# A conditioned block in fp32: two expert halves on VectorE, the second norm on ScalarE, pair sums and the last residual on GpSimd, and orders written out engine by engine

## The reference, cut to what matters

```python
mod = (_silu(L0_c) @ L0_wmod).reshape(8, 6, 1, -1)       # sa, ca, ga, sb, cb, gb per batch
ga = (2 * (ga >= 0) - 1) * jnp.maximum(jnp.abs(ga), 0.25)
gb = (2 * (gb >= 0) - 1) * jnp.maximum(jnp.abs(gb), 0.25)
h = _layernorm(x) * (1 + ca) + sa
# mixer: v, gate = split(h @ W_in + b_in); hs = scan(sigmoid(A) * hs + v); y = sigmoid(gate) * hs * C
x = x + ga * (y @ W_out + b_out)
h = _layernorm(x) * (1 + cb) + sb
# router: softmax(h @ gate_w + gate_b), weights under 0.1 dropped, the rest made to sum to 1
# experts: sum over 8 of weight[e] * (h @ expert_w[e] + expert_b[e])
x = x + gb * experts
```

## Time and profile before

| | |
|---|---|
| median of 3 runs | 230.62 us (230.43 to 231.8) |
| the profiled execution | 229.9 us, span of its instructions 227.9 us |
| VectorE busy | 210.7 us (92%) |
| TensorE busy | 205.3 us (90%) |
| ScalarE busy | 172.8 us (76%) |
| GpSimd busy | 155.7 us (68%) |
| granted TensorE clock, mean | 0.975 of 2.4 GHz |

### The profile page before, as it was taken

How to read it: one execution, slowest core, us unless ns; L and a number is a source line. 1 busy time by engine, 2 the same in 40 slices (tenths; PEclk the granted TensorE clock), 3 DMA queues, 4 the chain that set the end, 5 groups by cost and what they waited for, 6 DMA issues and landing times.

```text
span 227.9 us, 4259 instructions
## 1 busy us (share of the span) xinstructions
PE 205.3 (90%) x1013; PEld 148.4 (65%) x1013; DVE 210.7 (92%) x776; ACT 172.8 (76%) x558; POOL 155.7 (68%) x247
## 2 busy tenths in 40 slices
...
DMA packets 19217, 9.82 MB, mean 43 GB/s; under 512 B 1289, under 2 KB 19066, under 8 KB 19194
## 3 DMA queue, kind: packets, MB, share of 16 engines
...
...
## 4 chain that ended last, share of the span: by engine, by line
DVE 69%; issue 11%; PE 9%; ACT 7%; DMA 2%; POOL 1%; SPq 1%; DVEq 0%; ACTq 0%; POOLq 0%
DVE mix L740 10%; DVE hs L704 7%; DVE z L692 6%; DVE bn L584 5%; ACT z L485 5%; DVE bank_v L747 4%; DVE bn L577 4%; DVE x L760 4%; DVE x L721 4%; DVE var_e L609 3%; DVE mix L733 2%; DVE mean_var L595 2%; DMA x_in<-in_L_attn_x_dram 2%; DVE mean_var L597 2%; DVE bank_v L754 1%
## 5 line engine op out<-in xcount | busy, mean ns | idle before, releaser
L485 ACT ACTIVATE z<-ring,wts 128x128 f32<-128x128 f32 x448 | 123.3, 426 | 19.1 <-DVE wts L679 18.1
L376 POOL TENSOR_TENSOR z<-z 128x512 f32<-128x512 f32 x48 | 60.5, 1287 | 20.1 <-ACT z L485 20.1
L932 PE MATMUL ring<-expert_w_hi,h_hi 128*128 128x512 f32 x128 | 65.8, 514 | 1.7 <-ACT z L485 1.5
L355 POOL TENSOR_SCALAR xn<-x,neg_mean,rstd 128x128 f32<-128x128 f32 x64 | 27.7, 448 | 39.7 <-DVE rstd L636 39.7
L933 PE MATMUL ring<-expert_w_lo,h_hi 128*128 128x512 f32 x128 | 50.8, 397 | 0.0
L934 PE MATMUL ring<-expert_w_hi,h_lo 128*128 128x512 f32 x128 | 50.7, 396 | 0.0
L932 PEld LDWEIGHTS ring<-expert_w_hi,h_hi 128*128 128x128 f32 x128 | 24.6, 192 | 11.8 <-issue 9.4
L740 DVE TENSOR_REDUCE mix<-z 128x256 f32<-128x1024 f32 x16 | 31.6, 1974 | 0.3
L933 PEld LDWEIGHTS ring<-expert_w_lo,h_hi 128*128 128x128 f32 x128 | 24.6, 192 | 8.8 <-issue 6.5
L344 POOL TENSOR_SCALAR xn<-x_in,neg_mean,rstd 128x128 f32<-128x128 f32 x64 | 28.0, 451 | 2.9 <-DVE rstd L636 2.9
L934 PEld LDWEIGHTS ring<-expert_w_hi,h_lo 128*128 128x128 f32 x128 | 24.3, 190 | 5.6
...
## 6 DMA issues: line engine op xcount, KB each, us to landing
...
expert_b<-in_L_ffn_expert_b_dram SPq DMA_DIRECT2D x12, 4.0 KB
...
cond<-in_L_c_dram SPq DMA_DIRECT2D x1, 4.0 KB
```

The costliest lines, as they stand in the source:

```text
L355: last = nc.gpsimd.tensor_scalar(tile(xn2, g % 2, j), tile(x1, g % SLOTS, j), neg_mean[:, g % 2, j:j + 1], rstd[:, g % 2, j:j + 1], ALU.ad ...
L376: nc.gpsimd.tensor_tensor(z[:, g % 2, t, 0:4, :], z[:, g % 2, t, 0:4, :], z[:, g % 2, t, 4:8, :], ALU.add).then_inc(folded, 1)
L485: last = nc.scalar.activation(z[:, g % 2, t, e, :], bank_k[:, (e % 4) * P:(e % 4 + 1) * P], ACT.Copy, scale=wts[:, g % 2, t, e:e + 1])
L932: mm(bank_k[:, :], hi, expert_w_hi[:, cols], start=True, stop=False)
```

## The change

VectorE now takes two halves of each group, k = 5 and 7 (four of the last group). Tiles 2 and 3 then need no fold; GpSimd folds tiles 0 and 1 only, adds the pairs of both tile pairs, and VectorE ends each with a pair sum, so that no reduction over four is left. The second norm moves to ScalarE, as scale and bias, for which VectorE makes a `shift` of mean times inverse root (L990 of the new kernel). The scaling writes to a new SBUF tile `mixg`, and GpSimd adds the last residual (L451). In the fill, VectorE does the first two first norms and the first second norm. The last group is finished in two halves by VectorE, each stored by a DMA of its own. The condition and one bias row are loaded from ScalarE's queue, the gate bias goes through TensorE in one pass, as two rounded parts, and products come before their bias products. Halves take the four ring banks by turns in the order of the list. The orders are written out for each engine; steps 3 to 11 (TensorE), 2 to 11 (ScalarE), 1 to 11 (GpSimd) and 2 to 10 (VectorE) are still loops.

```diff
-DVE_HALF = 7
-BANK_OF_HALF = (1, 1, 0, 3, 3, 2, 0, 2)
+DVE_HALVES = (5, 7)
+LAST_DVE_HALVES = (1, 3, 5, 7)
+HALF_ORDER = ((7, 0), (3, 0), (4, 0), (0, 0), (1, 0), (2, 0), (5, 0), (6, 1))
...
+        def ring_bank(g, k):
+            return ring[place[g, k] % RING]
...
         @block.gpsimd
-            def second_norm(g):
...
+            def add_pairs(g, i):
+                wait_tile(pool, g, 2 * i)
+                wait_tile(pool, g, 2 * i + 1)
+                pair = slice(2 * i, 2 * i + 2)
+                nc.gpsimd.tensor_tensor(z[:, g % 2, pair, 0:2, :], z[:, g % 2, pair, 0:2, :],
+                                        z[:, g % 2, pair, 2:4, :], ALU.add).then_inc(pairs_added[i], 1)
+            def result(g):
+                pool.wait_ge(scaled, g + 1)
+                nc.gpsimd.tensor_tensor(x1[:, g % SLOTS, :], mixg[:, g % 2, :], x1[:, g % SLOTS, :],
+                                        ALU.add).then_inc(out_ready, 1)
...
+            for s in range(1, 12):
+                fold(s - 1, 1)
+                add_pairs(s - 1, 1)
+                add_pairs(s - 1, 0)
+                weight_parts(s)
+                first_norm(s + 4)
+                result(s - 1)
+                fold(s, 0)
...
         @block.scalar
+            def second_norm(g):
+                act.wait_ge(shift_ready, g)
+                for j in range(TILES):
+                    last = nc.scalar.activation(
+                        tile(xn2, g % 2, j), tile(x1, g % SLOTS, j), ACT.Identity,
+                        bias=shift[:, g % 2, j:j + 1], scale=rstd[:, g % 2, j:j + 1])
+                last.then_inc(xn2_ready, 1)
...
         @block.vector
             def times_gb(g):
                 dve.wait_ge(mix_ready, g + 1)
...
-                vec.tensor_tensor(by_tile(bank_v[:, :]), by_tile(bank_v[:, :]),
+                if g >= 2:
+                    dve.wait_ge(out_ready, g - 1)
+                vec.tensor_tensor(by_tile(mixg[:, g % 2, :]), by_tile(bank_v[:, :]),
                                   gb_all[:, g // per_batch:g // per_batch + 1, :].to_broadcast([P, TILES, P]),
                                   ALU.mult).then_inc(scaled, 1)
-            def result(g):
...
+            def shifts(g):
+                dve.wait_ge(mean_ready, g + 3)
+                dve.wait_ge(rstd_ready, g + 3)
+                vec.tensor_tensor(shift[:, g % 2, :], neg_mean[:, g % 2, 0:TILES], rstd[:, g % 2, 0:TILES],
+                                  ALU.mult).then_inc(shift_ready, 1)
...
+                weigh_onto(s - 1, 5, 0)
+                weigh_onto(s - 1, 5, 1)
+                weigh_onto(s - 1, 5, 2)
+                scan(s + 2)
+                gated(s + 2)
+                weigh_onto(s, 7, 0)
...
         @block.tensor
+            for s in range(3, 12):
+                state_input(s + 2, s - 2)
+                turn_xn2(s + 1)
+                turn_xn1(s + 3, s + 1)
+                half(s, 7)
+                half(s, 3)
+                output_product(s + 2, s + 3)
+                half(s, 4)
+                logits(s + 1)
...
+                gate_input(s + 3, s)
```

More of the change, by code:

```diff
@@ L514, in _ @@
+            parts_out(15)
         @block.vector
@@ new lines, in _ @@
+            root(-1, 6)
+            negated_mean(-1)
+            root(-1, 7)
+            first_norm(1)
+            x_stats(3, 0)
+            x_stats(2, 2)
+            x_stats(2, 3)
+            first_residual(0)
+            x_stats(3, 1)
+            x1_stats(0)
+            moments(0)
+            root(0, 0)
+            root(0, 1)
+            scan(1)
+            root(0, 2)
+            root(0, 3)
+            root(0, 4)
+            root(0, 5)
+            gated(1)
+            root(0, 6)
@@ new lines, in _ @@
+            negated_mean(0)
+            root(0, 7)
+            second_norm(0)
+            x_stats(4, 0)
+            x_stats(3, 2)
+            x_stats(3, 3)
+            first_residual(1)
+            x1_stats(1)
+            moments(1)
+            low_part(0)
+            root(1, 0)
+            x_stats(4, 1)
+            root(1, 1)
+            router(0, 0)
+            router(0, 1)
+            root(1, 2)
+            root(1, 3)
+            negated_mean(1)
+            root(1, 4)
+            router(0, 2)
@@ new lines, in _ @@
+            root(1, 5)
+            router(0, 3)
+            root(1, 6)
+            x_stats(4, 2)
+            router(0, 4)
+            root(1, 7)
+            router(0, 5)
+            shifts(1)
+            router(0, 6)
+            scan(2)
+            router(0, 7)
+            gated(2)
+            bias_parts()
+            x_stats(5, 0)
+            x_stats(4, 3)
+            first_residual(2)
+            x1_stats(2)
+            moments(2)
+            weigh_onto(0, 5, 0)
+            root(2, 0)
@@ new lines, in _ @@
+            moments(14)
+            negated_mean(14)
+            router(13, 1)
+            low_part(13)
+            root(14, 0)
+            weigh_onto(12, 5, 0)
+            sum_pairs(11, 0)
+            root(14, 1)
+            weigh_onto(12, 5, 1)
+            root(14, 2)
+            router(13, 2)
+            root(14, 3)
+            router(13, 3)
+            sum_pairs(11, 1)
+            router(13, 4)
+            root(14, 4)
+            weigh_onto(12, 5, 2)
+            router(13, 5)
```

1081 lines of the change are left out of this document (821 added, 260 removed).

## The result

The changed kernel takes 236.38 us, the median of 4 runs (236.04 to 236.55); the kernel before, beside it, 230.53 (229.99 to 231.8). The ratio is 1.024, with a 95% interval of 1.021 to 1.027. The forecast was 229.4, with a range up to 234.5. The profiled execution took 236.43 us, with a span of 234.6.

The account below looks back on a forecast made before the run. VectorE was taken to bound the kernel at 12.0 us a step, TensorE 0.2 behind. Residual 3 at 47.7, plus 149.4, 27.9 of drain and 2.4 of store gave span 227.4; 2.0 more made 229.4 us, range 218.5 to 234.5.

Parts of the forecast that it names:

- Up to group 0: Start of the kernel to the first residual addition: the new order gains nothing, residual 0 at 20.0 us.
- 0 to 1.5: Fill: us lost if TensorE comes in at 1.2 GHz with fewer fillers; counted in the range alone.
- Residual 1 to 3: Fill, between residuals of groups 1 and 3: 17.2 us of VectorE work plus 2.4 of waits, 19.6 for 23.1.
- The steady step: One step of the loop: VectorE's 10.8 plus 0.43, 1.2 and 0.1 of blocking, 12.5 us against 12.0.
- the 0.43 on the shift: Steady step: GpSimd's first norm instruction goes ahead of VectorE's shift, which loses 0.43 us.
- 1.2 on the weights: Steady step: the weights ask 0.1 us behind GpSimd's result and wait 1.2 us for it.
- Residual 3 to 15: Twelve steps between the residuals of groups 3 and 15: 149.4 us, against 143.5 before.
- Rival B: Steady step: the ports do not meet, step falls to TensorE's 11.6, total 220.4 us; chance 0.20.
- Rival C: Steady step: GpSimd's last pair addition runs late into the root, blocking var_e and guess; 235.4 us, chance 0.09.
- The drain: From residual 15 to the last result's end: 23.3 us of VectorE work plus GpSimd blocking, 27.9 against 29.6.
- the far price: Second norm on ScalarE: 0.43 us an instruction, GpSimd's price for the same norm; not taken, hidden either way.
- the near one: Second norm on ScalarE: 0.275 us an instruction, the price of a weighing; taken, hidden either way.

Follow-up runs that it names:

- a1: The changed kernel with one VectorE bn_stats moved behind the weights in steps 1 to 11, so the weights come one place earlier; 236.23 us, ratio 1.024.
- a2: The changed kernel with the turn of xn1(0) put ahead of gate_rows on TensorE, as before the change; 233.84 us, ratio 1.015.
- a4: The changed kernel with a second bn_stats put ahead of the weights in steps 1 to 11, so they ask later; 233.59 us, ratio 1.011.
- b2: The changed kernel with filler products added early on TensorE, four fewer in the turn of xn2(0), and xn1(0) turned ahead of gate_rows; 233.11 us, ratio 1.008.
- b3: The changed kernel with both the filler edit of b2 and the later scaling of b1; 232.27 us, ratio 1.004.
- d2: d1 with the turn of xn1(0) ahead of gate_rows and six filler products ahead of output_product(1); 227.94 us, ratio 0.979.
- e2: d2 with one multiply-add of half 5 and one bn_stats moved ahead of the scan; 229.21 us, ratio 0.982.
- d1: c1 with GpSimd's very first fold held back until VectorE has the weights of group 1; 230.35 us, ratio 0.992.
- c2: c1 with the filler of b2, and one multiply-add of half 5 and one bn_stats moved ahead of the scan; 228.09 us, ratio 0.983.
- b1: The changed kernel with the scaling (mixg) moved behind the weights in steps 2 to 11; 234.71 us, ratio 1.016.
- c1: The changed kernel with GpSimd's result of groups 0 to 11 waiting until VectorE has formed the weights two groups on; 228.39 us, ratio 0.991.
- b4: The changed kernel, unaltered, run once more on another chip; median 234.23 us, ratio 1.016.
- c3: The kernel before with only the scaling into mixg and the last residual on GpSimd, for all groups but the last; 239.98 us, ratio 1.040.
- after: The changed kernel as first measured, against the kernel before; 236.38 us, ratio 1.024.

## Why the prediction was wrong

- **The step that failed: "Up to group 0 the new order gains nothing ... and it comes to 20.0"**, with "0 to 1.5" of clock "in the range alone". Residual 0 came at 23.94, over half of the 7.2 us of span that the sum is short. Where the clock holds up to there (a1, a2, a4, b2, b3, d2, e2) it is at 19.5 to 20.2, so the order was read rightly. What was wrong is the price of the clock: TensorE at 1.2 GHz cost 3.4 us up to residual 0, where I had put at most 1.5 and nothing in the sum; the other 0.6 is the later wmod load. I took the price from a dip in the drain and did not ask what a late first grant would do to a chain in which TensorE, VectorE and ScalarE follow one another.
- **Residual 1 to 3, 19.6**, was 2.5 too low. Over these 22.1 us VectorE was busy 19.48 and idle 2.63, where I had 17.2 of work and 2.4 of waits: the waits were about right, the work was not. Of the work, 1.1 is the lock of the first fold on the weights of group 1 (1.28 for 0.17), which I had not placed; the other 1.2 I have not followed row by row. Taking the lock away gives back 0.5 (d1, d2). The filler is on this chain too: b2, b3 and c2, with four filler products fewer ahead of the turn of xn2(0), take 21.7 for 22.1.
- **The steady step, 12.5**, was right by its main mechanism: 12.44, wts at 1.22 for near 1.3, the result 0.1 before it; a4, b1 and c1 show the lock by itself. Of its parts the 0.43 on the shift was wrong (0.15, not blocked) and 1.2 on the weights came to 1.05; instead VectorE stood idle for 1.10 of 48 us, 0.28 a step, and the last 0.3 I have not traced. Residual 3 to 15 came to 149.7 for 149.4, partly by luck: the first ten steps took 124.6 for 125.5, the last two 25.1 for 23.9.
- **Rival B's price was wrong, and with it the bound.** B had 11.6 a step and 220.4 us once the ports do not meet, from TensorE's 11.83 less 0.2 to 0.3. That saving did not come: TensorE was busy 47.18 of 48 us before and 47.43 in c1, which is 11.74 a step in both, and the step is 11.9 (c1, e2). With the lock on the weights gone, the steady part wins 0.06 a step over the kernel before; what d2 gains lies at the ends: residual 3 comes 3.3 earlier, and from residual 15 to the span's end it takes 31.6 for 32.5 us.
- **Rival C** did not occur: var_e and guess last 0.16 and 0.17 in the steady step. Its 235.4 stood above the range's own end of 234.5, so the range was too narrow even by its own rivals. And luck has a part: on the second chip the same kernel took 234.23 (b4), just within the range, by an earlier clock alone as far as its trace shows.
- **The drain, 27.9**, came to 29.1: within the 30 that I had set. Its six parts add up to 23.5 and not 23.3, which makes 28.1. low_part 15, sum_pairs 13 and 14 and a fold_pairs met GpSimd as forecast. VectorE in the drain:

```profile
211.80 1.12 DVE L940 TENSOR_TENSOR h_lo<-h_t,h_hi 128x512 fp32r<-128x512 f32 x1 [0.44 <-ACT h_hi L570]
...
214.10 1.51 DVE L958 TENSOR_TENSOR mix<-z 128x256 f32<-128x256 f32 x1
...
217.51 1.51 DVE L958 TENSOR_TENSOR mix<-z 128x256 f32<-128x256 f32 x1
...
226.89 2.35 DVE L948 TENSOR_TENSOR z<-z 128x512 f32<-128x512 f32 x2
```

- **The norm on ScalarE**: 0.42 each by the page, so the far price (0.43) was the right one, not the near one (0.275). It hid, as forecast.

## What to carry to other kernels

Moving an elementwise addition from VectorE to GpSimd costs VectorE nothing only if none of the steps that the lock holds (here wts, with two operands in SBUF, and guess) asks while it runs; a small step that asks just behind it lasts 1.2 us instead of 0.2. Hold the GpSimd instruction back behind the small step (a wait for the weights) rather than move the small step, whose neighbours may free a buffer that another engine waits for. And a lock that is removed shows the next wait: price that one before promising the whole of it.

## What the runs showed of the chip

- The lock acts at a distance of 0.03 us (a1: 120.96, 120.99) as at 0.29 (a4), and it also holds a tensor_scalar step (guess, 1.20 in c3). A step that follows directly on one that GpSimd waits for gets through (the shift, 0.15, while GpSimd's norm instruction takes 0.56 for 0.45). In the steady steps of after, a bn_stats (0.28), the multiply-adds (0.33) and mixg (0.69), which read one operand from PSUM and one tile from SBUF, and the scan (1.26) run beside GpSimd at the length that they had before.
- The granted clock at the start is not a property of the kernel. The same TensorE stream ran at 2.4 GHz by 14 us and kept it for 11 us more (a1, a4), lost it again by 15 us (b4) or had it from 23 us on (after); TensorE, busy from 5.3 to 14.8 us, stayed at 1.2 GHz in after. Up to residual 0 that is worth as much as 3.4 us, and a single lot on one chip does not show it: the first four runs agreed within 0.5 us.
